# A linear-attention block with conditioning: its tensors laid out anew, its openings reordered, and the first batch's y computed from rounded parts

## The reference

```
xn = layernorm(x);  q = xn@Wq + bq;  k = xn@Wk + bk + (1-mask)*-1e6;  v = (xn@Wv + bv)*mask
q = softmax of q over the 64 features of a head;   k = softmax of k over the 2048 tokens
att = einsum('bnhd,bnhl->bhdl', k, v);   y = einsum('bnhd,bhdl->bnhl', q, att)
scale, shift = split(silu(cond)@W_emb + b_emb)
out = x + silu(layernorm(y)*(1+scale) + shift)@W_out + b_out
```

## Time and profile before

| | |
|---|---|
| median of 3 runs | 483.63 us (482.94 to 485.74) |
| the profiled execution | 484.99 us, of which the span of the instructions is 483.2 us |
| busy: PE, PEld, DVE, ACT, POOL | 464.2, 371.8, 363.3, 263.1, 132.8 us |
| PE's share of the chain that ended last | 83% |
| stages by start | opening 0 to 29 us, phase A to 123, first state to 170, phase C from 178 to 335, second state to 392, outputs to 480 |

### The profile page before, as it was taken

The page is one execution under the profiler, slowest core; times in us unless marked ns, Lnnn a source line. Parts: engine busy times, 40 slices in busy tenths (PEclk is TensorE's granted clock), DMA queues, the critical chain, the costliest instruction groups (busy, mean ns, idle before and its releaser), DMA issues.

```text
span 483.2 us, 7324 instructions
## 1 busy us (share of the span) xinstructions
PE 464.2 (96%) x2478; PEld 371.8 (77%) x2478; DVE 363.3 (75%) x879; ACT 263.1 (54%) x485; POOL 132.8 (27%) x148
## 2 busy tenths in 40 slices
PE   4999999998899999999999999999899999989997
PEld 2677876885688878888888888888588868878875
DVE  6979976775878956979678658675988628888963
ACT  5333332321788523347555655655988814777882
POOL 0013311120200000104223233332410133676675
PEclk9999999999999999999999999999999999999999
DMA  8945310112133200110213212121322000233354
GB/s 284 356 168 207 121 43 7 46 46 102 43 121 98 88 26 19 45 43 1 82 28 132 84 49 87 45 87 45 131 85 69 0 1 23 89 131 124 123 172 149
DMA packets 23093, 43.50 MB, mean 90 GB/s; under 512 B 1992, under 2 KB 2064, under 8 KB 23056
## 3 DMA queue, kind: packets, MB, share of 16 engines
q1 hardware_dynamic: 21968, 40.93, 24.7%
q10 hardware_dynamic: 1088, 2.10, 1.2%
HBM read 34.64 MB, written 8.39 MB: 89 GB/s over the span
## 4 chain that ended last, share of the span: by engine, by line
PE 83%; DVE 8%; ACT 3%; issue 3%; POOL 1%; DMA 1%; POOLq 0%; DVEq 0%; ACTq 0%
PE ps L1154 21%; PE ps L1156 21%; PE ps L1155 21%; PE ps L1159 8%; PE ps L1330 5%; ACT ps L407 2%; PE ps L1255 1%; PE ps L1308 1%; DVE th L916 1%; PE ps L1227 1%; PE ps L1208 1%; DMA x_in<-in_x_dram 1%; DVE yst_raw L661 1%; DVE kf L798 1%; DVE qs L762 1%
## 5 line engine op out<-in xcount | busy, mean ns | idle before, releaser
L577 POOL TENSOR_TENSOR qs<-qs,qmax 128x512 f32<-128x512 f32 x32 | 35.9, 1122 | 192.8 <-DVE qmax L767 192.8
L1154 PE MATMUL ps<-ek_hi,zm_hi 128*128 128x512 f32 x128 | 51.5, 402 | 3.7 <-DVE ek_lo L803 2.1
L1154 PE MATMUL ps<-wk_hi,zT_hi 128*128 128x512 f32 x124 | 51.5, 415 | 1.7 <-DVE kf L748 1.7
L1154 PE MATMUL ps<-wq_hi,zT_hi 128*128 128x512 f32 x128 | 52.3, 409 | 0.3 <-DVE qs L762 0.3
L1156 PE MATMUL ps<-wq_hi,zT_lo 128*128 128x512 f32 x128 | 50.6, 395 | 0.0
L1155 PE MATMUL ps<-wq_lo,zT_hi 128*128 128x512 f32 x128 | 50.5, 395 | 0.0
L306 ACT ACTIVATE zT_hi<-ps 128x512 fp32r<-128x512 f32 x32 | 19.1, 596 | 57.6 <-PE ps L1159 57.6
L1156 PE MATMUL ps<-ek_hi,zm_lo 128*128 128x512 f32 x128 | 50.4, 394 | 0.0
L1155 PE MATMUL ps<-ek_lo,zm_hi 128*128 128x512 f32 x128 | 50.3, 393 | 0.0
L1156 PE MATMUL ps<-wk_hi,zT_lo 128*128 128x512 f32 x124 | 49.0, 395 | 0.0
L1155 PE MATMUL ps<-wk_lo,zT_hi 128*128 128x512 f32 x124 | 49.0, 395 | 0.0
(11 more groups left out here) (230 smaller groups left out, 1163.2 us busy)
## 6 DMA issues: line engine op xcount, KB each, us to landing
x_in<-in_x_dram SPq DMA_DIRECT2D x32, 512.0 KB, 3.5
res<-in_x_dram SPq DMA_DIRECT2D x32, 256.0 KB, 2.8
out_dram<-res SPq DMA_DIRECT2D x32, 256.0 KB, 2.0
y<-in_L_cond_Wk_dram ACTq DMA_DIRECT2D x2, 512.0 KB, 5.3
kf<-in_L_cond_Wq_dram ACTq DMA_DIRECT2D x1, 1024.0 KB, 8.1
eq<-in_L_cond_W_out_dram SPq DMA_DIRECT2D x1, 1024.0 KB, 8.5
wv_mod<-in_L_cond_Wv_dram SPq DMA_DIRECT2D x1, 1024.0 KB, 10.7
eq<-in_L_cond_W_emb_dram SPq DMA_DIRECT2D x4, 256.0 KB, 4.4
```

What stands on the lines that cost most here:

```text
L577: pool.tensor_tensor(q_heads, q_heads, qmax[:].unsqueeze(2).broadcast_to([P, H, DH]), ALU.subtract).then_inc(s["q_shift"], 1)
L1154: pe.matmul(o, a[0], bb[0], start=start, stop=False)
```

## The change

The edits by place:

- The tensors are declared in another order: all large ones (x_in, zT, kf, eq, qs, km, zm, ek, y, eqT, u, th, res, att) stand right behind `part`, and all small ones (ones, pick, cols, lnb_w, pen, semb_t, emb_cols, ab, qmax, kcol, rz) behind them.
- `qs` and `qmax` are doubled. `q_add` waits for the exponential of two tiles ago in place of the last.
- Opening: `key_bias(1)` comes ahead of the first two `turn_z`; ScalarE makes `zT_high(0,0)` ahead of its wait for the second half of Wk and of `wk_high(2)`. ScalarE writes a scaled copy of each quarter of Wq into eq, and GpSimd subtracts the high part from it, in place of VectorE's four `weight_low` for wq. The second chunk of x statistics is kept in PSUM and finished ahead of the copy of the vectors, and `product_q(0,0)` waits for it.
- The second state's opening, the loops' `last_outputs` and one `silu` of the second batch's outputs are reordered. The first tiles of the rings wait for the last y product of batch 0.
- Residuals: those of the last eight tiles are loaded into x_in, in four transfers behind the last state product, and the tiles are added and stored there.
- y of batch 0: att and eqT are split in rounded high and low parts (`att_parts`, `eqT_low` on VectorE), and `product_y` makes 12 rounded matmuls of 130 or 128 columns per tile in place of 4 fp32 ones. `turn_q`, `turn_q_in_place` and `product_y` wait for `eqT_lo_ok` where they waited for `eqT_ok`. The low parts lie in the rings of the state, which is idle then.
- The last output tile is computed, added and stored in two halves of 256 columns.

The core of the diff:

```diff
...
         gT = y[:, 0:NB]
+        eqT_lo = zm_hi[:, 0:2, :].rearrange("p t (f c) -> p t f c", f=NB)
+        att_hi = ek_hi[:, 0:2, :].rearrange("p t c -> p (t c)")[:, 0:NB * YW].rearrange("p (q c) -> p q c", q=NB)
+        att_lo = zm_lo[:, 0, :].rearrange("p (q c) -> p q c", q=NB)
         den = km
...
             refill(HT - 1)
-            for m in range(HT, 2 * T):
+            sp.wait_ge(s["g_ps"], 2 * T)
+            for m in range(2 * T - XR, 2 * T, 2):
+                load_late(m)
...
                     refill(m - 1)
+            m = 2 * T - 1
+            for k in range(2):
+                c = slice(HD * k, HD * k + HD)
+                sp.wait_ge(s["o_ok"], m + 1 + k)
...
                     act.wait_ge(s["eqT_ps"], n + 1)
-                act.activation(eq[:, n, :], qs[:], ACT.Exp).then_inc(s["q_exp"], 1)
+                elif n < NB:
+                    act.wait_ge(s["wq_lo_ok"], n + 1)
+                act.activation(eq[:, n, :], qs[:, n % 2, :], ACT.Exp).then_inc(s["q_exp"], 1)
             def exp_k(b, n):
...
             normalise_x(0, 1)
+            zT_high(0, 0)
             act.wait_ge(s["wk_in1"], 16)
             wk_high(2)
-            zT_high(0, 0)
             wk_high(3)
...
                 wq_high(f)
+                copy(wq_scaled[:, f, :], wq_raw[:, f, :], "wq_scaled", ln_weight(f))
             act.wait_ge(s["bq_part"], 1)
...
             ek_high(1, 0)
-            scale_shift(HT)
             zm_high(1, 1)
...
             ek_high(1, 1)
+            scale_shift(HT)
             exp_q(1, T - 1)
-            h_high(HT)
-            scale_shift(HT + 1)
             def last_outputs(n):
-                if n == 2:
+                if n == 1:
+                    h_high(HT)
+                if n == 3:
+                    scale_shift(HT + 1)
+                if n == 5:
                     h_high(HT + 1)
...
                                pattern=[[-1, P]], channel_multiplier=1).then_inc(s["ident_ok"], 1)
+            for f in range(NB):
+                pool.wait_ge(s["wq_scaled"], f + 1)
+                pool.tensor_tensor(wq_lo[:, f, :], wq_scaled[:, f, :], wq_hi[:, f, :].bitcast(F32),
+                                   ALU.subtract).then_inc(s["wq_lo_ok"], 1)
...
                 dve.wait_ge(s["q_ps"], m + 1)
-                if m:
-                    dve.wait_ge(s["q_exp"], m)
-                dve.tensor_tensor(qs[:], ps[:, TB if m == 1 else QB, :], bq_all[:], ALU.add).then_inc(s["q_sum"], 1)
+                if m > 1:
+                    dve.wait_ge(s["q_exp"], m - 1)
+                dve.tensor_tensor(qs[:, n % 2, :], ps[:, TB if m == 1 else QB, :], bq_all[:], ALU.add).then_inc(s["q_sum"], 1)
             def q_top(b, n):
...
                 dve.wait_ge(s["q_sum"], m + 1)
-                dve.tensor_reduce(qmax[:], qs[:].rearrange("p (h d) -> p h d", h=H), AX_X,
+                dve.tensor_reduce(qmax[:, n % 2, :], qs[:, n % 2, :].rearrange("p (h d) -> p h d", h=H), AX_X,
                                   ALU.max).then_inc(s["q_max"], 1)
...
                                       rz[r, :].unsqueeze(2).broadcast_to([DH, NB, DH]), ALU.mult).then_inc(s["att_step"], 1)
+            def att_parts():
+                dve.wait_ge(s["att_step"], 2)
+                dve.tensor_copy(att_hi, att[:]).then_inc(s["att_hi_ok"], 1)
+                dve.wait_ge(s["att_hi_ok"], 1)
+                dve.tensor_tensor(att_lo, att[:, :, 0:P], att_hi[:, :, 0:P].bitcast(F32), ALU.subtract).then_inc(s["att_lo_ok"], 1)
+            def eqT_low(n):
+                dve.wait_ge(s["eqT_ok"], n + 1)
+                if n >= 2:
+                    dve.wait_ge(s["y_ps"], n - 1)
+                dve.tensor_tensor(flat(eqT_lo[:, n % 2]), ps[:, TB, :], flat(eqT[:, n % 2]).bitcast(F32),
+                                  ALU.subtract).then_inc(s["eqT_lo_ok"], 1)
             def y_tile(m):
...
             for f in range(NB):
-                weight_low(wq_lo, wq_raw, wq_hi, "wq", f)
                 x_tile_stats(0, 2 + f)
+            x_finish(0, 1)
             dve.wait_ge(s["vec_ps"], 2)
             dve.tensor_copy(cols[:, FIRST:ROWS], ps[:, YB + 1, 0:ROWS - FIRST]).then_inc(s["cols_ok"], 1)
-            x_finish(0, 1)
             dve.wait_ge(s["cols_ok"], 2)
...
             att_blocks(0)
+            eqT_low(0)
+            att_parts()
             for t in range(T):
...
                 if t < T - 1:
+                    eqT_low(t + 1)
                     q_add(1, t)
...
             k_less_max(1, 0)
+            masked_z(1, 1)
+            k_less_max(1, 1)
             out_tile(HT - 2)
-            k_less_max(1, 1)
             zm_low(1, 0)
...
             q_top(1, T - 1)
-            masked_z(1, 1)
+            out_tile(HT - 1)
+            zm_low(1, 1)
+            ek_low(1, 1)
             k_less_max(1, 2)
...
             silu(HT)
-            out_tile(HT - 1)
-            zm_low(1, 1)
-            ek_low(1, 1)
             def last_outputs(n):
-                if n == 1:
+                if 1 <= n < 5:
+                    y_finish(T - 1, (n - 1,))
+                if n == 5:
                     silu(HT + 1)
-                if 3 <= n < 7:
-                    y_finish(T - 1, (n - 3,))
                 if n == 10:
...
             y_tile(T + 7)
+            silu(T + 2)
             out_tile(HT + 3)
...
                     out_tile(m - 1)
-                if m + 2 < 2 * T:
+                if T < m < 2 * T - 2:
                     silu(m + 2)
...
-            out_tile(2 * T - 1)
+            m = 2 * T - 1
+            dve.wait_ge(s["res_b"], m + 1)
+            for k, bank in enumerate((o_bank(m), ps[:, YB, :])):
+                c = slice(HD * k, HD * k + HD)
+                dve.wait_ge(s["o_ps"], m + 1 + k)
+                dve.tensor_tensor(res_of(m)[:, c], bank[:, c], res_of(m)[:, c], ALU.add).then_inc(s["o_ok"], 1)
...
                     pe.wait_ge(s["gT_d"], 1)
+                if m == 0:
+                    pe.wait_ge(s["x_norm"], 2)
                 for f in range(NB):
...
                 if n:
-                    pe.wait_ge(s["eqT_ok"], n)
+                    pe.wait_ge(s["eqT_lo_ok"], n)
                 else:
...
                 if n < T - 2:
-                    pe.wait_ge(s["eqT_ok"], min(n + 4, T))
+                    pe.wait_ge(s["eqT_lo_ok"], min(n + 4, T))
                 if n and n < T - 2:
...
             def product_y(m):
-                pe.wait_ge(s["eqT_ok" if m < T else "eqT1_ok"], m % T + 1)
-                if m % T == 0:
-                    pe.wait_ge(s["att_step"], 2 * (m // T) + 2)
+                pe.wait_ge(s["eqT_lo_ok" if m < T else "eqT1_ok"], m % T + 1)
+                if m == 0:
+                    pe.wait_ge(s["att_lo_ok"], 1)
+                if m == T:
+                    pe.wait_ge(s["att_step"], 4)
                 if m and m <= T:
...
                     bank, at = y_bank(m) + q // 2, (q % 2) * YS
-                    last = pe.matmul(ps[:, bank, at:at + YW], eqT[:, m % 2, q, :] if m < T else blk(eq[:, m - T, :], q),
-                                     att[:, q, :], start=True, stop=True)
+                    if m < T:
+                        hi, lo = eqT[:, m % 2, q, :], eqT_lo[:, m % 2, q, :]
+                        pe.matmul(ps[:, bank, at:at + YW], hi, att_hi[:, q, :], start=True, stop=False)
+                        pe.matmul(ps[:, bank, at:at + P], hi, att_lo[:, q, :], start=False, stop=False)
+                        last = pe.matmul(ps[:, bank, at:at + YW], lo, att_hi[:, q, :], start=False, stop=True)
+                    else:
+                        last = pe.matmul(ps[:, bank, at:at + YW], blk(eq[:, m - T, :], q), att[:, q, :], start=True, stop=True)
                 last.then_inc(s["y_ps"], 1)
...
                     pe.wait_ge(s["wo_lo_ok"], NB)
+                if m == 2 * T - 1:
+                    pe.wait_ge(s["y_ok"], 2 * T)
+                    for k, bank in enumerate((o_bank(m), ps[:, YB, :])):
+                        c = slice(HD * k, HD * k + HD)
+                        for f in range(NB):
+                            last = split_product(bank[:, c], (blk(h_hi(m), f), blk(h_lo(m), f)),
+                                                 (wo_hi[:, f, c], wo_lo[:, f, c]), f == 0, f == NB - 1)
+                        last.then_inc(s["o_ps"], 1)
+                    return
                 for f in range(NB):
...
             key_bias(0)
+            key_bias(1)
             turn_z(0, 0)
             turn_z(0, 1)
-            key_bias(1)
             product_k(0, 0)
...
```

More of the change, by code:

```diff
@@ L31, in cond_linear_attention @@
     YS = 2 * P
+    HD = D // 2
     XR = 8
@@ L88, in cond_linear_attention @@
         part = sb("part", [P, P])
+        x_in = sb("x_in", [P, XR, D])
+        zT_hi, zT_lo = sb("zT_hi", [P, 2, NB, P], F32R), sb("zT_lo", [P, 2, NB, P], F32R)
+        kf = sb("kf", [P, T, D])
+        eq = sb("eq", [P, T, D])
+        qs = sb("qs", [P, 2, D])
+        km = sb("km", [P, D])
```

(27 more changed lines are left out.)

30 lines of the change are left out of this document (20 added, 10 removed).

## The result

The changed kernel takes 493.07 us (median of four runs, 492.46 to 494.36); the kernel before, run beside it, took 483.52 (482.94 to 485.74). The ratio is 1.0196, 95% interval 1.0166 to 1.0226: about 9.5 us slower. The forecast was 2.4 us slower, with a range that ended at 491; the direction was right, the size was not.

The account below looks back on a forecast made before the run. The prediction took TensorE's matmul stream as the bound, with 83% of the chain of waits. Its eight terms summed to +2.4 us, taking the profiled 484.99 to 487.4, or 486.0 beside the median 483.63; range 478 to 491.

Parts of the forecast that it names:

- Part 1: k, q and output products: with operands' offsets alike, the 512-column step gets shorter, -4.0 us.
- Part 2: First batch's y on TensorE: 12 rounded products at 0.12 us each replace 0.90 us a tile, +8.6 us.
- Part 3: VectorE in the first batch's y steps: late eqT_low makes in-place turns wait, mainly t=4 and 8, +5.0 us.
- Part 4: Second state's opening: the new order removes most TensorE waits and the fallen clock behind them, -3.2 us.
- Parts 5 to 8: Doubled qs, second batch's outputs, opening, last tile in halves with residuals: -1.3, -1.5, -0.7 and -0.5 us.
- rivals A and D: First batch's y: A, loads hidden, -3.3 in place of +8.6, 12%; D, load and stream in series, +17.5, 7%.
- rival C: k, q and output products: the offset is worth nothing, the kind of product sets the step; 490.0 us, 15%.
- Rival B: First batch's y steps: VectorE isn't late, its term costs 1 us in place of +5.0; 482.0 us, 20%.
- part 5: First state's opening: doubled qs ends q_add's wait for the exponential before it, -1.3 us.
- part 6: Second batch's outputs: silu(18) moved ahead ends TensorE's wait of 1.55 us at 428.39, -1.5 us.
- Part 8: End of the kernel: last output tile in halves and residuals in four transfers, -0.5 us.
- part 7: Opening: key_bias(1) fills TensorE's 0.66 us wait for the first x, the moved wq work stays hidden; -0.7 us.

Follow-up runs that it names:

- e4_offset: The kernel before with only the small tensors allocated behind the large ones: 480.34 us, ratio 0.9928.
- e3_early: The changed kernel with eqT_low(t+1) on VectorE ahead of the x statistics and k_tile of step t, not behind k_tile: 486.31 us, ratio 1.0049.
- e1_y32: The changed kernel with the first batch's y again as fp32 products, without eqT_low, att_parts and their waits: 478.62 us, ratio 0.9887.
- e7_oldstate: e1_y32 with the second state's opening and last_outputs in the order of the kernel before: 477.66 us, ratio 0.9866.
- e8_newstate: e1_y32 with a third order of the second state's opening, out_tile(10) ahead of keys_top, both masked_z ahead of both k_less_max: 476.49 us, ratio 0.9842.
- e6_gate: The changed kernel with GpSimd's h_low and add_bias (t of 5 and more) held back until VectorE's running maximum is done: 494.33 us, ratio 1.0209.
- e2_fill: The changed kernel with 13 unread matmuls of 512 columns ahead of the in-place turn of t=4, where TensorE stands idle: 493.50 us, ratio 1.0202.
- e9_cols: e3_early with the first batch's rounded y products cut to 66, 64 and 66 moving columns from 130, 128 and 130: 487.76 us, ratio 1.0080.
- e11_oldopen: e8_newstate with the opening of the kernel before (wq_lo on VectorE, key_bias(1) behind the turns of x): 475.51 us, ratio 0.9831.
- e5_bothoff: e4_offset plus a 32-byte tensor ahead of all others, so weights and turned tiles are both off by 32: 480.48 us, ratio 0.9929.

## Why the prediction was wrong

By its own steps, forecast and measured, in us:

| step | forecast | measured | from the ratios, times 483.5 |
|---|---|---|---|
| Part 1, offset | -4.0 | -3.5 | e4_offset |
| Part 2, y on TensorE | +8.6 | +7.8 | e3_early less e1_y32 |
| Part 3, VectorE late | +5.0 | +7.1 | the change less e3_early |
| Part 4, second state | -3.2 | +1.0 | e1_y32 less e7_oldstate |
| Parts 5 to 8 | -4.0 | -3.0 | e7_oldstate less e4_offset |
| sum | +2.4 | +9.4 | measured 9.5 |

**Part 4 failed, by 4.2 us**, the largest error, and twice over. "Both operands of step 1 ahead of silu(12)" was read for the products that it makes earlier, and not for the product that it makes later: out_tile(10) stands behind masked_z(1,1) and k_less_max(1,1), product_out(11) waits for it through `o_ok`, and that is TensorE's next instruction: 1.39 us. The queue was also counted at 0.6 us a step, and masked_z(1,1) took 1.36 and ek_lo(3) 1.77 beside GpSimd, as in the kernel before silu(12), ahead of out_tile(11), and ek_lo(1), which ended the wait of 1.33, had taken 1.80 and 1.77. How much of the waits this stretch makes no run at this place shows. In the kernel before, VectorE stood idle for 1.86 us ahead of keys_top and could have done out_tile(10) there, as e8_newstate does. And 1.5 of the 4.1 us to be gained was the clock at 0.50 behind the waits, a thing of the one profiled execution (484.99 us, granted clock 0.996): of the 31 runs of before beside the experiments, 21 with a clock of 1.00 take 482.8 to 484.6 us, and eight of 0.996 take 484.8 to 485.8. The sign that part 4 gave, no clock of 0.50 at the second state, did come true, but it does so without the new order as well, in e4_offset and e7_oldstate. The forecast took that cost away from the median, where it had not been; taking off 1.36 us to come to the median and counting the clock's 1.5 as a gain was the same money twice.

**Part 3 was right in place, cause and size of its waits** (3.08 and 1.72 us for 3.1 and 1.8, and 0.32 at t=2), and too small by 2.1 us for what follows them. I had read the low clock behind a wait in the earlier trace rows and priced it there, but not behind the wait that I forecast myself. Steps 4 and 5 together take 26.3 us in the changed kernel, 24.3 in e6_gate, where the clock doesn't fall, and 20.7 in e3_early. So in these executions the fall is worth about 2.0 us, and the waits 3.6. e2_fill, with 26.7, shows that keeping the clock at one place is not enough: TensorE meets VectorE again at t=5, and the clock may fall there.

**Part 2** was 0.8 too high: the step is 0.1125, not 0.12. The 0.1225 for the two-column pieces was taken from the 0.98 us of the chain of waits; by the timeline of the same trace they take 0.91 us to the next start, 0.114 each, the step of the fp32 pieces.

```profile
176.98 1.05 PE L1312 MATMUL ps<-part,km 128*128 128x2 f32 x8
177.89 0.63 PE L1159 MATMUL ps<-ident,eq 128*128 128x128 f32 x4
```

That streaming doesn't set the step was right (e9_cols), so rivals A and D are out. By the Trainium skill, TensorE: Matmul & The Clock Gate, Back-to-back issue gap, a pair of load and matmul at 128 columns takes about 81 ns; these runs, with fp32-rounded operands, show 112.

**Part 1** came out within 0.5 us, and rival C is out. Rival B, VectorE isn't late, would have been right with eqT_low in another place.

**Parts 5 to 8**, by stages from e4_offset to e7_oldstate: part 5 gave 1.5 us (the first state's stretch, 55.6 to 54.1; 1.3 forecast). The wait near 428 that part 6 is about is gone, and the outputs' stretch is 1.0 shorter although its last product is 0.2 longer: 1.2 of 1.5. Part 8 with its residuals gives 0.7, that 0.2 taken off, of the forecast 0.5, and part 7 nothing of 0.7 (e11_oldopen). These make 3.4; the ratios say 3.0, and the landing of the weights, which varies by more than that, can cover the difference.

## What to carry to other kernels

Price a new wait with what stands behind it: the clock that may fall, and the next place at which the late engine is late again. Filling the idle time gave nothing in the total; moving one instruction on the late engine gave 7.1 us. When an engine's order is changed, look for what the displaced instruction released, not only for what the promoted one does, and give an operation its time beside GpSimd, not its time alone. And a cost that one profiled execution shows and the median does not, like a fallen clock, is not there to be gained.

## What the runs showed of the hardware

- The step of a 512-column product in k and q, as the median over the tiles, is 0.229 us where both operands lie alike modulo 64 bytes (e4_offset and e5_bothoff) and 0.233 where they differ by 32 (before); both on and both off are the same (480.34 and 480.48 us).
- A VectorE operation with both operands in SBUF that starts while GpSimd works can stand still until GpSimd's operation is over: 0.69 us becomes 1.33 at t=8 in the changed kernel, and 0.69 again in e6_gate, where GpSimd comes later. masked_z(1,1), with one tensor and two columns from SBUF, takes 1.36 for 0.54 in the changed kernel. In e1_y32, additions that read PSUM, reductions and statistics took 0.69 beside GpSimd as well as alone. By the Trainium skill, SBUF — State Buffer, SBUF: two separate sides, the two engines share a port pair that one of them holds for its whole instruction, also when VectorE's operation has two SBUF inputs; the trace agrees.
- An idle time of 3.1 us ahead of the same instructions was followed by a granted clock of 0.50 in one execution and of 1.00 in another; 1.70 us by 0.50 in e2_fill, twice, and 1.72 by 1.00 in the changed kernel; and two waits of 1.0 and 1.3 us by 0.50 in e5_bothoff and by 1.00 in e4_offset. Over all executions the changed kernel's clock is 0.993 to 0.997, in four of four; e3_early's, which has one wait of 0.53 us in those steps, is 1.000 in six of six. What decides it behind one wait these runs don't show.
- A rounded product of 130, 128 or 66 columns with its own load takes 0.1125 us from one start to the next, one of 256 columns 0.12.
